# GpSimd splits 20 of the 32 heads of Wo beside the attention, and the last stage splits its first outputs before the weights

## What is computed

```
B, S, HID = 64, 32, 512;  D, HQ, HK = 128, 32, 8;  cache: 64 pages of 32 keys, 16 per sequence
q, k, v = x Wq', x Wk', x Wv'            # 32 query heads, 8 key and value heads
q, k = rope(rmsnorm(q)), rope(rmsnorm(k))
k_all, v_all = cache rows of the sequence's 16 pages, then the own 32 rows
o = softmax(mask(q k_all' / sqrt(D))) v_all          # 4 query heads share one key head
x = x + o Wo'                                        # Wo: 512 x (32*128)
x = x + x W' + 2 * lora of the 2 best of 8 experts   # L1, gates from logits plus a bias of the language id
x = x + (x W2' + b) + 2 * lora of the sequence's slot        # L2
x = x + lora of the sequence's slot                          # L3
```

## Time and profile before

| | |
|---|---|
| time, median of 3 runs | 2634.18 us (2633.91 to 2634.66) |
| the profiled execution's own time | 2633.39 us |
| its span, first to last instruction | 2631.6 us |
| TensorE busy in the span | 2530.8 us (96%) |
| VectorE, ScalarE, GpSimd busy | 1653.0, 1236.4, 742.3 us |
| mean granted TensorE clock | 0.989 of full speed |

### The profile page before, as it was taken

How to read it: one execution, slowest core, us unless ns; L and a number is a source line. 1 busy time by engine, 2 the same in 40 slices (tenths; PEclk the granted TensorE clock), 3 DMA queues, 4 the chain that set the end, 5 groups by cost and what they waited for, 6 DMA issues and landing times. The chain is left out here.

```text
span 2631.6 us, 48525 instructions
## 1 busy us (share of the span) xinstructions
PE 2530.8 (96%) x15312; PEld 2178.8 (83%) x15312; DVE 1653.0 (63%) x3906; ACT 1236.4 (47%) x3285; POOL 742.3 (28%) x783
## 2 busy tenths in 40 slices
PE   5899999999999999999999999999998799999998
PEld 4677777778799999999999999999997577777776
DVE  8999999992366666666666666666666433333332
ACT  5555555552355555555555555555555222222221
POOL 5877777773021111211112111122111200000000
PEclk9999999999999999999999999999999899999999
DMA  3233233236598888888888888888885222322221
GB/s 139 81 97 94 82 112 90 86 96 211 164 340 272 265 267 265 270 274 267 265 263 270 272 272 265 266 267 266 283 258 192 80 90 90 96 84 88 88 87 44
DMA packets 369851, 484.13 MB, mean 184 GB/s; under 512 B 50320, under 2 KB 304528, under 8 KB 366480
## 3 DMA queue, kind: packets, MB, share of 16 engines
q1 hardware_dynamic: 332816, 347.67, 42.6%
q0 software_dynamic: 36864, 134.23, 14.3%
HBM read 393.70 MB, written 88.08 MB: 183 GB/s over the span
## 5 line engine op out<-in xcount | busy, mean ns | idle before, releaser
L821 ACT ACTIVATE probs<-probs,neg_max 128x544 f32<-128x544 f32 x512 | 383.5, 749 | 559.2 <-DVE neg_max L870 559.2
L893 PE MATMUL s_bank<-k_t,q_t 128*128 128x288 f32 (+1 forms) x2048 | 556.5, 394 | 4.6 <-POOL v_own L784 3.6
L910 PEld LDWEIGHTS o_bank<-p_t,v_c 128*128 128x128 f32 x4096 | 537.5, 192 | 26.3
L910 PE MATMUL o_bank<-p_t,v_c 128*128 128x128 f32 x4096 | 539.7, 275 | 0.0
L839 DVE COPY p_t<-pt_a 128x256 f32<-128x256 f32 x512 | 217.9, 426 | 417.4 <-PE pt_b L921 417.4
L893 PEld LDWEIGHTS s_bank<-k_t,q_t 128*128 128x128 f32 x2048 | 350.2, 191 | 60.0 <-POOL v_own L784 4.1
L441 POOL TENSOR_TENSOR q_t<-normed,v_c 128x256 f32<-128x256 f32 x320 | 337.8, 1076 | 147.8 <-ACT normed L490 147.8
L870 DVE CUSTOM_DVE_ANT_0 probs<-s_bank,mask 128x544 f32<-128x544 f32 x512 | 367.1, 717 | 3.9 <-PE s_bank L893 3.9
L656 PE MATMUL acc<-w_hi,x_hi 128*128 128x512 f32 x768 | 318.0, 414 | 14.7 <-DVE x_lo L541 14.7
L657 PE MATMUL acc<-w_lo,x_hi 128*128 128x512 f32 x768 | 304.4, 396 | 0.0
L658 PE MATMUL acc<-w_hi,x_lo 128*128 128x512 f32 x768 | 303.1, 395 | 0.0
(11 more groups left out here) (128 smaller groups left out, 3739.4 us busy)
## 6 DMA issues: line engine op xcount, KB each, us to landing
k_t<-in_k_pages SPq DMA_DIRECT2D x1024, 128.0 KB
q_spill<-wo_early SPq DMA_DIRECT2D x32, 1024.0 KB, 5.1
q_t<-q_spill SPq DMA_DIRECT2D x64, 512.0 KB
o_spill<-o_t SPq DMA_DIRECT2D x64, 512.0 KB, 8.8
raw<-o_spill SPq DMA_DIRECT2D x64, 512.0 KB, 3.5
k_t<-in_w_qkv SPq DMA_DIRECT2D x12, 1024.0 KB, 7.9
k_spill<-wo_early SPq DMA_DIRECT2D x8, 1024.0 KB, 5.1
v_spill<-wo_early SPq DMA_DIRECT2D x8, 1024.0 KB, 4.8
```

What stands on the lines that cost most here:

```text
L821: nc.scalar.activation(probs[:, j % 4], probs[:, j % 4], ACT.Exp, scale=-1.0, bias=neg_max[:, j % 2:j % 2 + 1], accum_out=row_sum[:, j % 2 ...
L893: last = pe.matmul(s_bank[:, columns].rearrange("p (s t) -> p s t", t=PSIZE), q_t[:, par, g], k_t[:, par, slots, g], start=True, stop=True)
L910: last = pe.matmul(o_bank, values, p_t[:, i, c], start=c == 0, stop=c == KC)
```

## The change

GpSimd gets two more instructions behind the gathers of each of 20 sequences (`b` from 6 to 25): a cast of one head of Wo, 128x512, into a new buffer `hi_early`, and the subtraction that puts the lower half over that head in `wo_early`. So heads 0 to 19 are split inside `attend`, and `finish` keeps 6 pieces (heads 20 to 31) of which GpSimd subtracts two. ScalarE and VectorE split output chunks 0 and 1 first, then the pieces, with chunk 2 behind the third and chunk 3 behind the sixth. SP stores the outputs of sequence 62 ahead of `wo_late`; `load_weights` moves from `attend` into `finish`, behind chunks 2 and 3; the gathers of the adapters come after that. The language ids are repeated and laid out by the host as 128x16, so that one DMA of contiguous rows brings them in place of four.

```diff
+HI_EARLY = 20
+SPLIT_FROM = 6
...
+        hi_early = nc.alloc_sbuf_tensor_at("hi_early", [P, HI_EARLY, D], F32R, offset=hi_start(nc))
...
+                for c in range(2):
+                    load_chunk(sp, 0, c)
+                store(B - 2, 0)
                 load_first(sp)
-                store(B - 2, 0)
                 sp.wait_ge(summed, (B - 1) * HK)
-                load_weights(sp)
                 store(B - 1, 1)
...
+                def split_weights(h):
+
+                    pool.wait_ge(wo_in, 16 * (WO_EARLY // HS))
+                    nc.gpsimd.tensor_copy(hi_early[:, h], wo_early[:, h]).then_inc(hi_early_done, 1)
+                    pool.wait_ge(hi_early_done, h + 1)
+                    nc.gpsimd.tensor_sub(lo_early[:, h], wo_early[:, h], hi_early[:, h].bitcast(F32)).then_inc(early_split, 1)
...
                         gather_values(pool, par)
+                        if SPLIT_FROM <= b < SPLIT_FROM + HI_EARLY:
+                            split_weights(b - SPLIT_FROM)
...
-                for a in range(TB):
-                    sp.dma_start(lang_i[S * a:S * (a + 1), :], lang[a::TB].partition_broadcast(S),
-                                 allow_slow_non_contiguous=True).then_inc(lang_in, 16)
+                sp.dma_start(lang_i[:, :], lang).then_inc(lang_in, 16)
                 follow_chunk(0, 2)
+                follow_chunk(0, 3)
+                load_weights(sp)
                 sp.wait_ge(slots_in, 16 * 2)
                 gather(0, 0, False)
                 gather(0, 1, False)
-                follow_chunk(0, 3)
...
+                for c in range(2):
+                    upper(0, c)
                 act.wait_ge(wo_in, 16 * (WO_EARLY // HS))
-                for k in range(WO_PIECES):
+                for k in PIECES:
...
-                    if k % NCH == 1:
-                        upper(0, k // NCH)
+                    if k in CHUNK_AFTER:
+                        upper(0, CHUNK_AFTER[k])
...
-        "lang": a["itok_B_0_7"],
+        "lang": np.repeat(a["itok_B_0_7"], S).reshape(NT, P).T,
```

More of the change, by code:

```diff
@@ L672, in attend @@
 def attend(nc, sem, ident, seq_f, pages, page_row, in_page_i, key_index, q_t, k_t, v_c, qk_in, v_in, v_named, wo_early,
-           wo_in, stored, o_stored, loads, load_first, load_weights, wo_t, v_dram, o_dram):
+           wo_in, lo_early, hi_early, hi_early_done, early_split, stored, o_stored, loads, load_chunk, load_first, wo_t,
+           v_dram, o_dram):
     UNITS = 2 * HK
@@ L1017, in finish @@
         WO_PIECE = 2
-        WO_PIECES = HQ // WO_PIECE
-        POOL_EVERY = 4
+        FIRST_PIECE = HI_EARLY // WO_PIECE
+        PIECES = range(FIRST_PIECE, HQ // WO_PIECE)
+        POOL_PIECES = (FIRST_PIECE + 1, FIRST_PIECE + 5)
+        CHUNK_AFTER = {FIRST_PIECE + 2: 2, FIRST_PIECE + 5: 3}
         def of_heads(early, late, h0, h1):
@@ L1034, in wo_lower, with split_before @@
             h0, h1 = k * WO_PIECE, (k + 1) * WO_PIECE
-            return of_heads(lo_early, lo_late, h0, h1), wo_raw(k), wo_hi[:, h0:h1].bitcast(F32)
+            return of_heads(lo_early, lo_late, h0, h1), wo_raw(k), hi_late[:, h0 - HI_EARLY:h1 - HI_EARLY].bitcast(F32)
+        def split_before(pieces, k):
+            return sum(i <= k for i in pieces)
+        DVE_PIECES = [k for k in PIECES if k not in POOL_PIECES]
         with nc.Block() as block:
@@ L1110, in _ @@
                 pool.wait_ge(own_set, 2 + 2 * TB)
-                for k in range(POOL_EVERY - 1, WO_PIECES, POOL_EVERY):
-                    pool.wait_ge(wo_hi_done, k + 1)
+                for k in POOL_PIECES:
+                    pool.wait_ge(wo_hi_done, k - FIRST_PIECE + 1)
                     low_half, whole_piece, high_half = wo_lower(k)
@@ L1268, in chain @@
                         lower(t + 2, 0)
-                for k in range(WO_PIECES):
-                    if k % POOL_EVERY != POOL_EVERY - 1:
-                        dve.wait_ge(wo_hi_done, k + 1)
+                for c in range(2):
+                    lower(0, c)
+                for k in PIECES:
+                    if k in DVE_PIECES:
+                        dve.wait_ge(wo_hi_done, k - FIRST_PIECE + 1)
                         low_half, whole_piece, high_half = wo_lower(k)
                         nc.vector.tensor_tensor(low_half, whole_piece, high_half, ALU.subtract).then_inc(wo_split, 1)
-                    if k % NCH == 1:
-                        lower(0, k // NCH)
+                    if k in CHUNK_AFTER:
+                        lower(0, CHUNK_AFTER[k])
                 dve.wait_ge(expert_set, 1)
-                dve.wait_ge(lang_in, 16 * TB)
+                dve.wait_ge(lang_in, 16)
                 nc.vector.tensor_copy(expert[:, :], expert_i[:, :]).then_inc(lang_set, 1)
```

49 lines of the change are left out of this document (27 added, 22 removed).

## The result

| | before | after |
|---|---|---|
| median | 2634.05 us (4 runs, 2631.14 to 2634.66) | 2612.97 us (4 runs, 2612.14 to 2613.67) |
| profiled execution, its span | 2633.39, 2631.6 us | 2612.14, 2610.3 us |
| TensorE busy | 2530.8 us | 2526.3 us |
| VectorE, ScalarE, GpSimd busy | 1653.0, 1236.4, 742.3 us | 1635.9, 1225.6, 777.7 us |
| granted clock | 0.989 | 0.993 |

The ratio is 0.9922, with an interval of 0.9905 to 0.9939. The forecast was 2607.2 us with a range of 2603.5 to 2618: the time is in the range, and 5.8 us above the forecast.

What follows compares the result with a forecast made beforehand. TensorE bounds the kernel, with 26 us of idling at the border between attention and last stage. Gains of 24.6 and 3.0 us less 0.5 in the attention give -27.0, from 2634.18 to 2607.2 us; range 2603.5 to 2618.

Steps and rivals of the forecast that it cites:

- The start: Start of the last stage: TensorE begins at 2020.75, 2.3 us earlier, after 3.7 us of idling.
- Four chunks without a stop, to 2045.5: Last stage: TensorE runs chunks 0 to 3 unbroken, ending at 2045.5 against 2067.7 before.
- its deadline of 2032: Last stage: chunk 2's data must have landed by 2032; landing was forecast at 2027, or 2031 at 300 GB/s.
- the 13.8 forecast: Last stage: chunks 0 and 1 together take 13.8 us on TensorE, the clock having fallen in the idle time before.
- The lower half of (1, 0) ready by 2043.4: Ahead of the tile-0 chain: VectorE's subtraction of (1, 0) waits for GpSimd until 2042.2 and ends at 2043.4.
- the 2.97 us that were to go: First chain, tile 0 to tile 1: the slow clock's 2.97 us go, as TensorE idles under 1 us there.
- The attention at 0.5 us: Attention: GpSimd's added work in 20 sequences costs 0.5 us in all, by holding VectorE's L847.
- the cover: Attention: L847 may be held 0.6 us, from L870's end to the next score's weight load, without delaying TensorE.
- Rival (d): Attention: VectorE's L870 is held too and a split sequence costs over 1.9 us; slower, say 2644 us; chance 0.03.

Runs made afterwards that it cites:

- weights_early: The changed kernel with W1, W2 and the bias asked for in the attention again, ahead of the last store: 2616.2 us, ratio 0.9935.
- split_ahead: The changed kernel with GpSimd's cast and subtraction of each head ahead of the four gathers in place of behind them: 2613.88 us, one execution.
- tile1_first: The changed kernel with chunk (1, 0) asked for ahead of the 16 gathers: 2606.55 us, ratio 0.9905.
- after_again: The changed kernel unaltered, timed again on a chip where all kernels took about 4% longer: 2721.89 us, ratio 0.9896.
- the quarters: The changed kernel with GpSimd's subtractions of W1 and W2 in four parts each: 2720.69 us; with chunk (1, 0) also ahead of the gathers: 2723.64 us.

## Why the prediction was right, and where it was 5.8 us off

**The start.** Forecast 2020.75, measured 2021.13, with a wait of 3.81 for the 3.7 forecast. Right; the attention had ended 0.3 us later than before, a shift that is there at 720 us already and in the kernel of the ids alone too, so not a price of the split.

**Four chunks without a stop, to 2045.5.** Measured 2045.06. Chunk 2 landed at 2030.6, not 2027, inside its deadline of 2032; some 1 us of slack was left (its lower half was ready at 2033.0, TensorE came to it at 2033.93), and `weights_early` shows the wait that comes when it is used up. Chunks 0 and 1 took 12.8 us for the 13.8 forecast, as the clock came back sooner than in the pair that the 13.8 was read from; in `split_ahead` they took 13.95. This 1.0 us was luck.

**The lower half of (1, 0) ready by 2043.4.** This is the step that failed. It had the chunk cast by 2041.2 and VectorE getting in at the gap between W1 and W2. GpSimd's W1 ended near 2044.9, not 2042.2. W1 and W2 had landed by 2035.2, as forecast, but the cast of W1 waits for a semaphore that counts the bias too, the last of that group in the queue: asked for at 2026.63, it landed 11.7 us later, at 2038.3, and ScalarE idled 2.80 us for it. The prediction had no term for that. As an estimate from the rows: cast from 2035.5 on, with W1 ready after 1.9 us and twice 4.6 us on GpSimd, W2 would have ended near 2046.6 and the add come some 2.8 us earlier; no run tried it. Nor was there a term for the landing of (1, 0). The gathers ahead of it started at 2030.37, not near 2026; it was asked for at 2038.62, landed at 2044.3, and missed even the later gap by 0.6 us. The add came 4.86 us late (2050.41 for 2045.55), the engine idled 6.18 us, and the clock fell: the window from 2050 to 2054 shows 0.50, and the next period has 1.8 of the 2.97 us that were to go. `tile1_first` shows it: with the chunk early the add stands at 2045.06 and the next 35.48 later. Which side of the gap the chunk falls on is a race that the unchanged code won in `after_again`, so the step was not wrong in kind, but it was a throw of tenths of a us and not the settled wait that it was taken for.

**The attention at 0.5 us.** Measured 0.0 over the split sequences. The reason was right in kind: L867 is held when GpSimd's subtraction comes first (1.36 and 1.26 us), the cover is 0.55, and in the changed kernel the gather ends just late enough that L867 starts beside the end of the cast and the subtraction waits for it (1.45 in place of 1.28 us). Even the small hold by the cast did not come. Rival (d) falls with L890, 0.72 us beside a subtraction of GpSimd.

**What no step had.** The new buffers cost 0.16 us per tile (+2.2), and the clock in the last tile was kinder by 2.8 us in this execution, which is luck: without it the time would have been near 2615.8, still in the range. Added to the forecast of -27.0: +4.9 for the add, +2.0 for the slow clock and the first of those periods, +2.2, -0.5 of the attention, -2.8 for the tail give -21.2, the measured -21.25.

## What to carry to other kernels

Look behind a late transfer at what stands ahead of it in its queue, in number of elements and not in bytes: one edit of 8 KB of ids was two thirds of the gain. An engine that is idle can take work for nothing if its instructions fall where they hold nobody up, so the phase has to be read, and where it can't be fixed, short instructions keep a hold short (a chunk's subtraction took 2.09 us at most beside the quarters, and up to 5.5 beside a whole weight). Look at what a semaphore counts: a small load at the end of a group can hold up the large one that is there already. And once the front of a stage is closed up, the next chunk in the same queue is the late one: ask for it before the small gathers.

## What was not expected of the hardware

A DMA of the language ids, 32x16 elements of 4 bytes, took the queue 1.5 to 2.7 us to issue (four in 5.82 or 10.89), and the 512 KB chunk behind four of them landed after 20.5 and 23.5 us, against 9.9 at most in the changed kernel. The Trainium skill (DMA: Bandwidth & Descriptors, Rules for kernel authors) says that a last dimension that isn't contiguous becomes one descriptor for each element; the packets under 512 B fell from 50320 to 48352 with the edit, 1968 fewer for 2048 ids, which agrees.

The same matmul of 128x512 took 2 ns more on average (427 for 425, 395 for 393) with its operand in the new buffers. The clock in the last tile fell for longer in some executions than in others with the same work, and the tail varied from 25.6 to 28.8 us; and two profiles of one kernel differ by 5 us in a single wait, since a data arrival decides on which side of a gap of GpSimd an instruction of VectorE falls.
